# Four V' products of a tile in one run, and the second projection's rotation and square behind other work, in a fused two-stack transformer kernel

## What is computed

```
qkv = x @ Wqkv;  q, k, v of 16 heads of 64
q = l2norm(q) * q_scale;  k = l2norm(k) * k_scale;  rotary embedding on q and k
P = softmax(8 * q @ k^T) over windows of 32 tokens and the window before
x = x + (P @ v) @ Wo
x = x + (a * gelu(gate)) @ W2 + b2,  with [a, gate] = layernorm(x) @ W1 + b1
```

## Time and profile before

| | |
|---|---|
| median of 3 runs | 3688.96 us (3684.85 to 3690.24) |
| the profiled execution's own time | 3686.52 us |
| its span, first to last instruction | 3684.7 us |
| busy share of the span | PE 93%, DVE 77%, ACT 65%, POOL 63% |
| mean granted clock of TensorE | 0.970 of full speed |
| the chain that ended last | PE 86%, issue 4%, DVE 4%, ACT 3% |

### The profile page before, as it was taken

One profiled execution on the slowest core, in us unless ns is written; L12 is line 12 of the kernel. 1 busy time (PEld: TensorE's weight loads), 2 busy tenths in 40 slices (PEclk: granted clock), 3 DMA queues, 4 the chain that ended last, 5 costly groups with the idle time before them and its releaser, 6 DMA issues.

```text
span 3684.7 us, 129395 instructions
## 1 busy us (share of the span) xinstructions
PE 3433.7 (93%) x51660; PEld 1855.8 (50%) x51660; DVE 2845.5 (77%) x6042; ACT 2381.3 (65%) x4153; POOL 2333.4 (63%) x2187
## 2 busy tenths in 40 slices
PE   3799999999999999999797999999999999999997
PEld 2355554554554554555363555545545545545553
DVE  1788887887887887888367888878878878878883
ACT  1576776775776776677524667767767766766774
POOL 0677766766766776767145767667667766767661
PEclk6899999999999999999998999999999999999999
DMA  5000000000000000000100000000000000000000
GB/s 187 10 9 28 21 12 27 22 12 27 21 13 27 21 12 25 24 12 5 54 1 8 11 26 23 12 27 21 13 27 21 12 27 22 12 24 26 12 5 13
DMA packets 50151, 83.62 MB, mean 23 GB/s; under 512 B 7168, under 2 KB 37120, under 8 KB 47232
## 3 DMA queue, kind: packets, MB, share of 16 engines
q1 hardware_dynamic: 49536, 75.05, 6.5%
HBM read 67.69 MB, written 7.34 MB: 20 GB/s over the span
## 4 chain that ended last, share of the span: by engine, by line
PE 86%; issue 4%; DVE 4%; ACT 3%; POOL 1%; DMA 1%; SPq 0%; DVEq 0%; ACTq 0%; POOLq 0%
PE VS L890 19%; PE QA L830 18%; PE TB L849 10%; PE TB L914 7%; PE VS L937 7%; PE TB L873 6%; PE FB L963 3%; PE FB L964 3%; PE FB L972 3%; PE VS L928 2%; ACT KT L460 2%; PE TB L857 1%; PE FB L948 1%; PE FB L953 1%; DMA KT<-in_w_out 1%
## 5 line engine op out<-in xcount | busy, mean ns | idle before, releaser
L334 POOL TENSOR_TENSOR QN<-T 128x512 f32<-128x512 f32 x768 | 980.0, 1276 | 673.6 <-DVE T L606 673.6
L341 POOL TENSOR_TENSOR QN<-QN,RR 128x512 f32<-128x512 f32 x768 | 801.6, 1044 | 316.8 <-DVE RR L627 316.8
L830 PE MATMUL QA<-WQ,Y 128*128 128x512 f32 x1536 | 806.3, 622 | 68.7 <-DVE T L606 25.4
L890 PE MATMUL VS<-MW,Y 128*32 128x512 f32 x6144 | 738.8, 598 | 2.7 <-DVE Z L679 2.7
L446 ACT ACTIVATE SQ<-QA 128x512 f32<-128x512 f32 x768 | 458.6, 597 | 289.3 <-PE QA L830 254.5
L606 DVE TENSOR_TENSOR T<-QA,TAB 128x256 f32<-128x256 f32 x1536 | 571.0, 412 | 4.1 <-issue 4.1
L601 DVE TENSOR_TENSOR T<-QA,TAB 128x512 f32<-128x512 f32 x768 | 522.9, 681 | 48.2 <-issue 21.3
L466 ACT ACTIVATE V<-VS 128x512 f32<-128x512 f32 x768 | 461.1, 600 | 90.1 <-PE VS L890 89.5
L633 DVE TENSOR_TENSOR Y<-TB,Y 64x128 f32<-64x128 f32 x384 | 111.0, 289 | 521.0 <-PE TB L857 518.3
L614 DVE TENSOR_REDUCE SSQ<-SQ 128x8 f32<-128x512 f32 x768 | 486.8, 675 | 0.0
L914 PEld LDWEIGHTS TB<-CST,QN 128*128 128x128 f32 x3072 | 360.9, 142 | 220.9 <-issue 183.5
(11 more groups left out here) (172 smaller groups left out, 4260.2 us busy)
## 6 DMA issues: line engine op xcount, KB each, us to landing
TAB<-in_tables SPq DMA_DIRECT2D x192, 128.0 KB, 2.1
WQ<-in_w_qk SPq DMA_DIRECT2D x48, 256.0 KB, 3.2
MW<-m_dram SPq DMA_DIRECT2D x12, 1024.0 KB, 4.8
m_dram<-QN SPq DMA_DIRECT2D x6, 1024.0 KB, 4.9
W1R<-in_w SPq DMA_DIRECT2D x12, 341.0 KB, 3.4
KT<-in_w_vt SPq DMA_DIRECT2D x6, 512.0 KB, 5.8
KT<-in_w_out SPq DMA_DIRECT2D x6, 512.0 KB, 6.6
W<-in_w SPq DMA_DIRECT2D x12, 192.0 KB, 2.4
```

The costliest lines, as they stand in the source:

```text
L334: po.tensor_tensor(QN[:, n % 2, k, :], T1[:, k, :], T2[:, k, :], ALU.add).then_inc(s_add, 1)
L341: po.tensor_tensor(heads(QN[:, m % 2, k, :]), heads(QN[:, m % 2, k, :]), RR[:, m % 2, 8 * k:8 * k + 8].unsqueeze(2).to_broadcast([P, 8, DH ...
L830: mm(QA[:, k % 2, :], Y[:, j * P:(j + 1) * P], WQ[:, k, :], start=True, stop=True).then_inc(s_qk, 1)
L890: last = mm(VS[32 * q:32 * q + 32, w % 2, :], Y[:, a:a + WIN], MW[:, q, :], start=True, stop=True, tile_position=(0, 32 * q), skip_group_c ...
```

## The change

TensorE: all four V' products follow the second half of the transposition of P, so `out_transpose`, the second projection and all behind them come after V' products 2 and 3. ScalarE: `square(0)` stands ahead of the copy of the attention's output, the exponential stands directly behind `p_out`, all four `v_out` follow it in one run, and `square(1)` comes behind them. VectorE: `rotate(1)` and `square_sum(1)` stand behind the softmax's sums and reciprocals. No instruction is added or removed, and all waits keep their places with their instructions.

```
@@ ScalarE, slot @@
+                if live(c, 0, it):
+                    square(0)
                 if live(c, 5, it):
                     m = n - 5
                     ac.wait_ge(s_o, by_tile(1, m, it, 1))
                     nc.scalar.activation(ON[:, m % 2, :], TB[:, 1, 0:P], ACT.Copy).then_inc(s_oe, 1)
                 if live(c, 4, it):
                     p_out(4, 1)
-                    v_out(0)
-                if live(c, 0, it):
-                    square(0)
-                if live(c, 4, it):
-                    v_out(1)
-                if live(c, 0, it):
-                    square(1)
                 if live(c, 3, it):
                     m = n - 3
                     ac.wait_ge(s_z, by_tile(1, m, it, 1))
                     nc.scalar.activation(Z[:, m % 2, :], Z[:, m % 2, :], ACT.Exp, scale=8.0).then_inc(s_ex, 1)
+                if live(c, 4, it):
+                    v_out(0)
+                    v_out(1)
+                    v_out(2)
+                    v_out(3)
+                if live(c, 0, it):
+                    square(1)
                 if live(c, 1, it):
                     qk_out(1, 0)
                     qk_out(1, 1)
-                if live(c, 4, it):
-                    v_out(2)
                 if live(c, 0, it):
                     square(2)
-                if live(c, 4, it):
-                    v_out(3)
-                if live(c, 0, it):
                     square(3)
@@ VectorE, slot @@
                 if live(c, 0, it):
                     rotate(0)
-                    rotate(1)
                     square_sum(0)
-                    square_sum(1)
...
                     nc.vector.reciprocal(RC[:, m % 2, :, :], SM[:, m % 2, :, :]).then_inc(s_rc, 1)
                 if live(c, 0, it):
+                    rotate(1)
+                    square_sum(1)
                     rotate(2)
                     square_sum(2)
                     square_sum(3)
@@ TensorE, slot @@
                 if live(c, 4, it):
                     p_transpose(4, 1)
-                    project_v(0)
-                    project_v(1)
+                    for w in range(4):
+                        project_v(w)
                 if live(c, 5, it):
                     out_transpose()
...
                     qk_transpose(1, 0)
                     qk_transpose(1, 1)
-                if live(c, 4, it):
-                    project_v(2)
-                    project_v(3)
                 if live(c, 0, it):
                     project_qk(2)
```

More of the change, by code:

```diff
@@ L496, in slot @@
                     p_out(4, 1)
[L497 to L503, removed]
                 if live(c, 3, it):
```

## The result

The changed kernel takes 4531.86 us (median of 4 runs, 4520.31 to 4538.82) against 3689.6 us before: 1.228 times, 95% interval 1.225 to 1.231. Forecast were 4409 us in a range of 4224 to 4570. The direction and the range held; of the 842 us lost the sum had 720.

The account below looks back on a forecast made before the run. TensorE, busy 93%, was taken to bound the kernel, in a circle of waits with VectorE. To the profiled 3686.5 us came 595 for the order and 125 for the clock, 4407, plus 2.4 to the median: 4409 us, range 4224 to 4570.

Parts of the forecast that it names:

- the sum: Three engine parts, 12.94 us per four slots over 46 fours: 595 us; the clock term adds 125 us.
- What bounds: TensorE, busy 93%, bounds; VectorE's idle time is free only where it stands, in a circle of waits with TensorE.
- part 1 and 2 (the circle): From output transposition's start (zero), later rotation 1 delays the fourth projection, 4.22 us per four slots; V' products ahead cost 6.88.
- Part 3 (the exponential): On ScalarE the exponential delays the copy V' product 2 needs: 0.46 us a slot, 1.84 in four, 85 us in all.
- The clock: After long TensorE waits the clock falls to 1.2 GHz: 83 of 138 slots at 1.5 us, 125 us; bounds 0 and 235.
- The case that I gave 0.15: Rival: the clock falls in nearly every long-wait slot, 4519 us, or 4570 with copies late too; chance 0.15.
- The rival that ends faster: Rival: rotation 1 done within 3.0 us after zero, so only saved run ends count, 24 to 46 us, about 3655; chance 0.02.

Follow-up runs that it names:

- in two pairs: Kernel of 3627 us with its run of four V' products parted again by the transpositions of q and k, all else in place: 3679.47 us.
- the run in another place: Kernel before with four V' products in one run behind output transposition and second projection, ScalarE reordered to suit, VectorE's order as before: 3626.91 us, ratio 0.984.

## Why the prediction was right, and where it was off

- **What bounds, and part 1 and 2 (the circle).** Right, nearly to the hundredth: the fourth projection starts 6.40 us after zero for 6.41, and 5.73 for 5.75 in the slots with c % 4 = 0 and 1 (medians of the trace). VectorE's free 2.7 us a slot were free only where they stood.
- **Part 3 (the exponential).** Right: 2.19 for 2.18 us from product 0 to product 2; 84.8 us for 85 where the clock is up in both kernels, 69 in the changed kernel itself.
- **The sum without the clock.** It had 595 us. The run that does the third projection twice has the clock back and shows 4318 - 3690 = 628. In its trace the slots with c % 4 = 1, 2, 3 and 0, from one output transposition to the next, take 19.19, 21.74, 20.27 and 19.61 us, 13.5 more in all than before, where the sum had 12.94. Two terms are short. A projection that begins after a wait takes 1.12 us for its two passes, not 1.02 (rows at 721.11 and 695.24), about 0.1 a slot. And for c % 4 = 3 ScalarE comes late out of gelu and its table load: there `p_out` starts 0.28 us after product 0 instead of 0.10, and V' product 2 starts 2.37 us after product 0, not 2.19. The rule of the Trainium skill (Perfetto Trace Analysis, Matmuls), that groups rotating through banks hide the copies, did not hold for this order: the wait of 0.4 us a slot stands in the trace, and goes once the exponential is behind copy 1. The copies are short enough, their place is not.

```profile
735.44 1.28 ACT L485 ACT_TABLE_LOAD   x1
...
736.73 0.60 ACT L446 ACTIVATE SQ<-QA 128x512 f32<-128x512 f32 x1
737.10 1.92 PE L887 MATMUL VS<-MW,Y 128*32 128x512 f32 x16
...
737.38 0.60 ACT L472 ACTIVATE PT<-TB 128x512 f32<-128x512 f32 x1
...
739.47 1.92 PE L887 MATMUL VS<-MW,Y 128*32 128x512 f32 x16 [0.44 <-ACT V L466]
```

- **The clock.** The mechanism was right, the size was off; this is the term of the sum that was mis-sized. I took six of ten long waits at 1.5 us, 125 us; it was 214 (4531.9 - 4318.0). Both factors were too low. By the granted clock in the traces, the changed kernel has 145 stretches at the lower level, 787 us in all, and the one with the doubled projection 32, 255 us in all. That is 113 more where I had 83, at 214 / 113 = 1.9 us each where I had 1.5. Counted by waits: of the 138 waits of over 2 us for the rotation, 121 had the clock come down during them or within 1.5 us behind them. My bound of 1.7 us a fall was none, since it took every fall to last the 3.4 us of the earlier trace rows; 37 of the 121 lasted twice as long or more, and the 113 are 4.7 us long on average (533 / 113).
- **Why so often** was not tested. Single waits behind the loop's turns brought the clock down in two of four, but there a full run of products came right before the pause, and here a pause of 0.3 to 1.0 us and one projection.
- **Luck in the range.** The case that I gave 0.15, the clock down in nearly every such slot, names what happened, and its 4519 us lie only 13 from the measured time; but that is in part two errors that cancel, a sum 33 us too low and a clock term 21 too high (235, from too many falls at too low a price). The upper end of 4570 does not follow from its terms either: 4519 and 184 copies that are late by 0.34 more make 4582.
- **Power and batches.** The rule of the Trainium skill (Perfetto Trace Analysis, Matmul Optimizations), that power follows utilization, agrees with these traces as far as the clock shows it: 0.913 with the pauses, 0.971 with them filled. What it says of batches did not help the V' run, whose gain of some 50 us has nothing to do with the clock (0.970 with it, 0.971 in two pairs).
- **The rival that ends faster** had its price right in kind (24 to 46 us for the ends of a run; 50 to 53 measured), but its condition was far from met: 5.73 us where it needed 3.0. With the run in another place it is met, and the gain is real.

## What to carry to other kernels

When two engines release each other in one slot, the idle time of the one that does not bound is slack of a circle: before moving a step, add up the path around it from the release to the need, in both orders. Put the short step that releases another engine ahead of the long work that nobody waits for, here 0.17 us ahead of four products, worth 738 us. And a pause of TensorE can have to be paid twice: here one of 2.2 us a slot brought the clock down behind it in 121 of 138 cases, and 165 us of useless work that filled it made the kernel 214 us faster.

## What the runs showed of the hardware

- TensorE came down from the 2.4 to the 1.2 GHz level during or right behind 121 of the changed kernel's 138 waits of over 2 us for the rotation, nearly all with a shorter pause and a single projection before them, and 2 of its 57 waits of 1 to 2 us. With 0.86 us more of work in the pause it was 1 of 136 waits of 1 to 2 us; the mean clock is 0.913 against 0.971.
- A fall of the clock lasted 3.4 us in 84 and 6.8 us or more in 37 of the 121 cases, and cost 1.9 us on average.
- Two passes of a projection that begins after a wait take 1.12 us, back to back 1.02, and the next can start 0.96 us behind them instead of 0.86 (rows at 695.24, 692.87 and 691.91 of the run with the third projection twice).
- Parting a run of products on 32 columns by full transpositions costs 0.26 to 0.27 us for each extra run (3679.47 against 3626.91 us).
